# Recommender forward pass on one core: the next chunk's features loaded into X1's low half, a fourth weight slot, and three moves inside a step

## The reference

```python
target = item_id_feat + item_img_feat
x = concat([t, seq_emb, t - seq_emb, t * seq_emb], axis=-1)      # 50 history rows per item
weights = softmax(where(mask, -1e9, relu(x @ aw1 + ab1) @ aw2 + ab2), axis=1)
hist_feat = einsum('bs,bsd->bd', weights, seq_emb)
se = sparse * sigmoid(relu(z @ se_w1 + se_b1) @ se_w2 + se_b2)[:, :, None]   # 5 fields
vids = einsum('bfd,fde->bfe', se[:, :4], bil_W)
p = [vids[:, i] * se[:, j] for i in range(4) for j in range(i + 1, 5)]       # 10 pairs
dnn_in = concat([se, p])                                          # 15 features of 128
for i in range(2):                                                # cross_K is 2 x 1920 x 1920
    xc = dnn_in * (xc @ cross_K[i] + cross_bias[i]) + xc
h = gelu(ln(xc @ w1 + b1)); h = gelu(ln(h @ w2 + b2)); out = sigmoid(h @ w3 + b3)
```

## Time and profile before

| | |
|---|---|
| median of three runs | 2404.17 us |
| profiled execution, its span | 2398.13 us, 2396.1 us |
| TensorE busy | 2011.4 us, 84 % |
| VectorE, ScalarE, GpSimd busy | 1332.8, 902.6, 882.1 us |
| first product of chunk 0, 1, 2, 3 | at 403.2, 905.4, 1448.9, 1982.6 us |
| DMA | 220.33 MB, 92 GB/s over the span |

### The profile page before, as it was taken

How to read it: one execution, slowest core, us unless ns; L and a number is a source line. 1 busy time by engine, 2 the same in 40 slices (tenths; PEclk the granted TensorE clock), 3 DMA queues, 4 the chain that set the end, 5 groups by cost and what they waited for, 6 DMA issues and landing times. The chain is left out here.

```text
span 2396.1 us, 33252 instructions
## 1 busy us (share of the span) xinstructions
PE 2011.4 (84%) x9609; PEld 1554.4 (65%) x9609; DVE 1332.8 (56%) x2211; ACT 902.6 (38%) x1954; POOL 882.1 (37%) x854
## 2 busy tenths in 40 slices
PE   2654645999999988989989987989999988999995
PEld 1433433777766766767767766767767766888884
DVE  3434444576676644565676644566677644445542
ACT  1333322444444323554444323554444333322222
POOL 5666666565555500545565500445650000000000
PEclk6656565999999998999999998999999999999997
DMA  4111111334343442233343443233342343233330
GB/s 135 43 39 42 40 41 52 108 107 114 108 118 105 123 124 81 83 84 114 95 119 104 118 128 91 79 86 111 105 115 83 89 124 96 87 95 95 99 90 10
DMA packets 124354, 220.33 MB, mean 92 GB/s; under 512 B 22272, under 2 KB 50704, under 8 KB 124048
## 3 DMA queue, kind: packets, MB, share of 16 engines
q1 hardware_dynamic: 69440, 148.69, 20.9%
q0 software_dynamic: 27136, 55.63, 9.0%
q10 hardware_dynamic: 27600, 13.90, 2.1%
HBM read 205.27 MB, written 12.85 MB: 91 GB/s over the span
## 5 line engine op out<-in xcount | busy, mean ns | idle before, releaser
L386 POOL DMA_INDIRECT e<-in_item_table,idx_all x800 | 828.2, 1035 | 868.8 <-POOLq L404 386.3
L1011 DVE TENSOR_TENSOR Wl<-raw,Wh 128x640 fp32r<-128x640 f32 (+1 forms) x420 | 338.1, 805 | 315.4 <-DVEq L1010 287.4
L734 ACT ACTIVATE Wh<-raw 128x640 fp32r<-128x640 f32 (+1 forms) x420 | 300.5, 721 | 488.4 <-ACTq L733 427.2
L498 PE MATMUL xps<-X0h,Wh 128*128 128x512 f32 x900 | 375.2, 417 | 36.1 <-PEq L496 25.0
L498 PE MATMUL xps<-X1h,Wh 128*128 128x512 f32 x900 | 364.4, 405 | 11.6 <-PEq L492 6.3
L500 PE MATMUL xps<-X0h,Wl 128*128 128x512 f32 x900 | 360.8, 401 | 0.0
L499 PE MATMUL xps<-X0l,Wh 128*128 128x512 f32 x900 | 360.5, 401 | 0.0
L499 PE MATMUL xps<-X1l,Wh 128*128 128x512 f32 x900 | 354.5, 394 | 0.0
L500 PE MATMUL xps<-X1h,Wl 128*128 128x512 f32 x900 | 354.3, 394 | 0.0
L428 PE MATMUL aps<-ident,e 128*128 128x128 f32 x800 | 142.0, 318 | 173.7 <-issue 89.7
L702 ACT ACTIVATE e<-e,pw 128x128 f32<-128x128 f32 x800 | 242.7, 388 | 14.9 <-ACTq L128 11.7
(11 more groups left out here) (134 smaller groups left out, 2185.6 us busy)
## 6 DMA issues: line engine op xcount, KB each, us to landing
raw<-in_cross_K SPq DMA_DIRECT2D x360, 320.0 KB
raw<-in_w SPq DMA_DIRECT2D x60, 256.0 KB
e<-in_item_table,idx_all POOLq DMA_INDIRECT x800
dnn_scratch<-dn ACTq DMA_DIRECT2D x12, 960.0 KB
raw<-dnn_scratch SPq DMA_DIRECT2D x45, 256.0 KB
dn<-in_embT SPq DMA_DIRECT2D x1, 1024.0 KB
img_scratch<-dn ACTq DMA_DIRECT2D x1, 1024.0 KB, 5.2
S<-img_scratch ACTq DMA_DIRECT2D x16, 64.0 KB
```

The lines of the kernel that those rows point to most:

```text
L386: nc.gpsimd.indirect_dma_start(out=dst, out_offset=None, in_=table, in_offset=bass.IndirectOffsetOnAxis(ap=idx_all[:, t, s:s + 1], axis=0) ...
L498: m0 = mm(out, wh, Xh[:, k, 0:nb], start=(k == 0), stop=False)
L734: af(Wh[:, split_slot(w), 0:n], raw[:, rs, 0:n], ACT.Copy).then_inc(hi_done, 1)
L1011: v.tensor_tensor(Wl[:, rs, 0:n], raw[:, rs, 0:n], Wh[:, slot, 0:n].bitcast(F32), ALU.subtract).then_inc(lo_done, 1)
```

## The change

Six things change.

1. **Features.** `X1l` now lies on a float32 buffer `x1f`, and `X0l` on `x0f`, each with the layout [partition, tile, feature, item] where it was [partition, feature, 512 items]. A layer's new features are formed in place in `x1f` or `x0f`; `xnew` is gone. When the last feature of layer 1 is formed, X1 isn't needed any more, and ScalarE issues two loads (`rows_load`) that bring all 15 features of the next chunk to `x1f`: features 0 to 7 (2 MB) and 8 to 14. They are split from there by a table, two of them in w1 step 4, two in step 5, and so on. The SyncE queue carries weights alone.
2. **Layout.** The moving operand of every cross matmul is now four runs of 128 columns, and VectorE's and ScalarE's operations on a chunk are 128x4x128. A tile's store to DRAM and its high and low split in the opening are contiguous.
3. **Rings.** `RING` 3 to 4, `WRING` 5 to 6, and weights are split three blocks ahead, not two. The descriptor scratch of GpSimd goes from 8192 to 4096 bytes.
4. **Plan.** For tiles that are not in the opening: `fetch` at s-6, `aim` at s-4, `swing` at s-1 (the step without a group).
5. **TensorE's step.** `tail_turn` stands at the end of its step, `tail_bilinear` in the next step behind the first part. `fc_turn2` and `fc_w3` stand behind the second part.
6. **ScalarE's step.** `tail_copy` is first in the step after the turn, `tail_store` is last but for `fc_sd`, the head's second gelu stands behind the second copy of the group. On VectorE `fc_logits` stands one part later, and the low halves signal TensorE without a wait of VectorE on itself.

```diff
-RING = 3
-WRING = 5
+RING = 4
+WRING = 6
+LOOK = RING - 1
@@ make_plan
-        plan[s - 3].aim = plan[s - 2].swing = plan[s - 1].share = plan[s].neg = t
-        plan[max(s - 5, 0)].fetch = t
+        if t < TILES[0]:
+            fetch, aim, swing = max(s - 5, 0), s - 3, s - 2
+        else:
+
+            fetch, aim, swing = s - 6, s - 4, s - 1
+        plan[fetch].fetch = plan[aim].aim = plan[swing].swing = plan[s - 1].share = plan[s].neg = t
...
+LOADS = ((0, 8), (8, FEATS))
+SPLITS = {4: (0, 1), 5: (2, 3), 6: (4,), 7: (5,), 8: (6,), 9: (7,), 10: (8, 9), 11: (10,), 12: (11,), 13: (12,), 14: (13,)}
@@ build
-        dnn_d = nc.dram_tensor("dnn_scratch", (FEATS, P, ntiles, P), F32, kind="Internal").ap()
+        dnn_d = nc.dram_tensor("dnn_scratch", (ntiles, P, FEATS, P), F32, kind="Internal").ap()
-        X0l = sb("X0l", [P, FEATS, NB], F32R)
-        X1l = sb("X1l", [P, FEATS, NB], F32R)
+        x1f = sb("x1f", [P, TPC, FEATS, P])
+        x0f = sb("x0f", [P, TPC, FEATS, P])
+        X1l = nc.alloc_sbuf_tensor_at("X1l", [P, TPC, FEATS, P], F32R, offset=x_at)
+        X0l = nc.alloc_sbuf_tensor_at("X0l", [P, TPC, FEATS, P], F32R, offset=x_at + 4 * TPC * FEATS * P)
@@ TensorE, products
-                    m0 = mm(out, wh, Xh[:, k, 0:nb], start=(k == 0), stop=False)
+                    m0 = mm(out, wh, Xh[:, 0:T, k, :], start=(k == 0), stop=False)
@@ TensorE, step
                 products(p.chunk, p.layer, p.n, 0)
                 if T and 2 <= k < T + 2:
                     fc_turn1(k - 2)
-                if T and k == T + 3:
-                    fc_turn2(pairs(T)[0])
...
                 if p.open:
                     hidden()
-                if p.lift is not None:
-                    tail_turn(p.lift)
+                if p.pair is not None:
+                    tail_bilinear()
                 if p.grp:
                     transposes(*p.grp, 0)
 
                 products(p.chunk, p.layer, p.n, 1)
                 if p.grp:
-                    transposes(*p.grp, 1, p.swing is not None)
+                    transposes(*p.grp, 1)
                 elif p.swing is not None:
                     head_turn()
+                if T and k == T + 3:
+                    fc_turn2(pairs(T)[0])
...
                 products(p.chunk, p.layer, p.n, 2)
...
-                if p.lift is not None:
-                    tail_bilinear()
                 if p.open:
                     score()
+                if p.lift is not None:
+                    tail_turn(p.lift)
@@ ScalarE
+            def rows_load(c):
+                act.wait_ge(x1_free, 1).then_inc(x1_free, -1)
+                act.wait_ge(dnn_stored, DMA * (BASE[c] + TILES[c] - TILES[0]))
+                for i, (a, b) in enumerate(LOADS):
+                    act.dma_start(x1f[:, 0:TILES[c], a:b, :],
+                                  dnn_d[BASE[c]:BASE[c] + TILES[c], :, a:b, :].rearrange("t p f b -> p t f b")).then_inc(rows_landed[i], DMA)
@@ ScalarE, w1_stage
-                    if c + 1 < CHUNKS and k:
-                        r_hi(c + 1, k - 1)
+                    if c + 1 < CHUNKS:
+                        if k == 0:
+                            rows_load(c + 1)
+                        for r in SPLITS.get(k, ()):
+                            r_hi(c + 1, r)
@@ kernel
-    nc = bacc.Bacc("TRN2", target_bir_lowering=False, num_devices=1, dynamic_dma_scratch_size=8192)
+    nc = bacc.Bacc("TRN2", target_bir_lowering=False, num_devices=1, dynamic_dma_scratch_size=4096)
```

More of the change, by code:

```diff
@@ L269, in build @@
         w_free = sem("w_free")
-        r_free = sem("r_free")
+        x1_free = sem("x1_free")
+        rows_landed = [sem(f"rows_landed{i}") for i in range(2)]
         split_free = sem("split_free")
@@ L325, in build @@
         opening, chunks = make_plan()
-        order = load_order()
-        raw_slot = {item: i % WRING for i, item in enumerate(order)}
         TOTAL = CHUNKS * STREAM
@@ L337, in span, with by_tile, fresh @@
             return TILES[c] * P
+        def by_tile(x, c):
+            return x.rearrange("p (t b) -> p t b", b=P)[:, 0:TILES[c], :]
+        def fresh(c, layer, n):
+            return (x1f, x0f)[layer][:, 0:TILES[c], n, :]
         def e_sub(g, u, s):
@@ L355, in _ @@
             sp.dma_start(w2[:], w2_d.rearrange("(k p) n -> p k n", p=P)).then_inc(late_in, DMA)
[L356 to L358 removed]
+            for w in range(TOTAL):
+                if w >= WRING:
                     sp.wait_ge(w_free, 1).then_inc(w_free, -1)
[L360 to L371 removed]
+                b = w % STREAM
+                src = kx_d[b] if b < BLOCKS else w1_d[(b - BLOCKS) * P:(b - BLOCKS + 1) * P, :]
+                sp.dma_start(raw[:, raw_slot(w), 0:width(w)], src).then_inc(raw_landed[raw_slot(w)], DMA)
             sp.wait_ge(res_ready, 1).then_inc(res_ready, -1)
@@ L598, in step @@
                     fc_turn1(k - 2)
+                if p.open:
+                    hidden()
+                if p.pair is not None:
+                    tail_bilinear()
+                if p.grp:
+                    transposes(*p.grp, 0)
+                products(p.chunk, p.layer, p.n, 1)
+                if p.grp:
+                    transposes(*p.grp, 1)
+                elif p.swing is not None:
+                    head_turn()
                 if T and k == T + 3:
@@ L604, in step @@
                     fc_w3(T)
-                if p.open:
-                    hidden()
-                if p.lift is not None:
-                    tail_turn(p.lift)
-                if p.grp:
-                    transposes(*p.grp, 0)
-                products(p.chunk, p.layer, p.n, 1)
-                if p.grp:
-                    transposes(*p.grp, 1, p.swing is not None)
-                elif p.swing is not None:
-                    head_turn()
                 products(p.chunk, p.layer, p.n, 2)
@@ L799, in step @@
                     r_hi(c, FEATS - 1)
+                if p.pair is not None:
+                    tail_copy(p.pair)
                 unit(c, 3 * k)
@@ L817, in step @@
                     fc_gelu1(k - 2)
+                if p.grp:
+                    copy_eT(1)
+                elif p.swing is not None:
+                    copy_tT(p.swing)
                 if T and k == T + 3:
@@ L848, in _ @@
                 if p.k == 6:
-                    w_hi(0)
-                    w_hi(1)
+                    for w in range(LOOK):
+                        w_hi(w)
             for c in range(CHUNKS):
@@ L1136, in step @@
                 if prev:
-                    x_sum(c, prev[2])
+                    x_sum(*prev)
                 if p.summed:
@@ L1172, in step @@
                 unit_out(c, 3 * k + 2)
+                if T and k == T + 5:
+                    fc_logits(c - 1)
                 if p.gate is not None:
@@ L1202, in w1_stage @@
                         x_lo(c, 1, FEATS - 1)
-                    if c + 1 < CHUNKS and k:
-                        r_lo(c + 1, k - 1)
+                    if c + 1 < CHUNKS:
+                        for r in SPLITS.get(k, ()):
+                            r_lo(c + 1, r)
             dve.sem_inc(bank_free, BANKS)
@@ L1227, in _ @@
                 if p.k == 6:
-                    for w in range(2):
+                    for w in range(LOOK):
                         w_lo(w)
```

138 lines of the change are left out of this document (54 added, 84 removed).

## The result

| | before | after |
|---|---|---|
| median | 2405.28 us (2397.41 to 2407.41, 4 runs) | **2236.61 us** (2234.53 to 2242.17, 4 runs) |
| profiled execution, its span | 2398.13 us, 2396.1 us | 2237.56 us, 2235.5 us |
| first product of chunks 0, 1, 2, 3 | 403.24, 905.37, 1448.94, 1982.61 us | 408.72, 870.02, 1353.07, 1832.03 us |
| cross layers of chunks 0 to 3 | 443.2, 484.6, 474.6, 327.0 us | 420.5, 441.7, 438.2, 318.0 us |
| w1 stage to the next chunk's first product | 58.9, 59.0, 59.1 us | 40.8, 41.4, 40.8 us |

The ratio is 0.931 with the interval [0.928, 0.934]: 168.7 us faster, where 141 were forecast. The time lies just under the low end of the range, so what follows has to find some 28 us (168.7 less 141.1) that the sum had in no term.

What follows compares the result with a forecast made beforehand. GpSimd's gathers pace the opening; from 403 us TensorE decides, with 149 us of gaps. Terms summed to 141.1 us off the profiled 2398.1, giving 2257.0; with 6.0 for the median, 2263 us, range 2238 to 2320.

Steps and rivals of the forecast that it cites:

- w1 stages and chunk starts: TensorE's weight waits in w1 stages, 23.8 us gained; waits and slow matmuls at a chunk's first products, 37.6 us.
- turn: Steps 9, 15 and 21: nine TensorE waits for ScalarE's copy of the fields, with 49 slow matmuls, go; 37.7 us.
- store and target: Store last and `aim` a step earlier take 18 TensorE waits summing to 19.7 us; 16 us gained.
- one more weight: Splitting weights one block further ahead (the lookahead) removes weight waits inside steps; 20 of 21.8 us gained.
- head: `fc_turn2` behind the second part takes two waits and 6 slow matmuls, 7.7 us; 6 us gained.
- opening: Paced by GpSimd's gathers, unchanged; smaller scratch costs nothing, first product of chunk 0 still near 403 us.
- layout: 5400 cross matmuls reading their moving operand in four runs cost nothing; bounds zero to 2,600 us.
- rival A: Waits are moved, not removed: half of turn, store, one more weight and head comes back, 40 us; 2303 us, chance 0.16.
- The landing: First feature load on chip 20.2 us into the w1 stage, leaving TensorE about 0.5 us late for weight 8.
- Rival B: In w1 stages the feature loads starve the weights, 25 us a chunk, 75 in place of 4.5; 2333 us, chance 0.11.
- Rival C: Slower than before: TensorE pays for each jump in its moving operand; 2425 us at 10 ns a jump, chance 0.04.
- Rival D: No gain: TensorE's gaps are there for another reason than read; chance 0.02.

Runs made afterwards that it cites:

- features alone: Kernel before with the features' two large loads, layout, scratch 4096 and the low halves' new signal; rings, plan and step order as before: 2257.91 us, ratio 0.950.
- signal alone: Kernel before with one edit, the low half of a new feature (`x_lo`) signals TensorE itself: 2335.79 us, ratio 0.983.
- turn back: Kernel after with the fields transposed ahead of the group's transposes, their copy later, and the bilinear product at the step's end again: 2244.37 us, ratio 0.944.
- store back: Kernel after with the tile's store ahead of the second copy to `eT` again: 2217.37 us, ratio 0.933.
- plan back: Kernel after with `aim` at s-3, `swing` at s-2 and `fetch` at s-5 again: 2210.56 us, ratio 0.930.
- rings back: Kernel after with `RING` 3 and `WRING` 5, weights split two blocks ahead again: 2222.08 us, ratio 0.936.
- features and rings: Kernel after without the moves (also "no moves"): plan, turn, store and head order as before, features and rings as after: 2258.42 us, ratio 0.950.
- scratch 4096: Kernel before with GpSimd's descriptor scratch at 4096 bytes in place of 8192, nothing else: 2380.12 us, ratio 1.001.

## Why the prediction was right, and where its sum was off

Its picture of what bounds the kernel held: TensorE's gaps decided, the w1 stages lost theirs, the 5 us at a chunk's start and the waits at the turn in steps 9, 15 and 21 went, and no rival decided. Chunks 0 to 2 with their w1 stages are 156 us shorter, where under 100 would have been the sign of being wrong. The sizes are off in both directions, and one source of gain was missed.

| term | forecast, us | measured, us | from |
|---|---|---|---|
| w1 stages and chunk starts | 23.8 + 37.6 = 61.4 | 81 to 86 | features alone: 52.6 + 3 x 9.4, with or without 5 for the first groups |
| VectorE's own wait and signal behind `x_lo` | not priced | 38 | signal alone |
| turn | 37.7 | 33 | turn back |
| store and target | 16 | 4 one by one, 10 with the head | store back, plan back; turn back against no moves |
| one more weight | 20 | 9.5, or 0 without the moves | rings back, features and rings |
| head | 6 | its waits were moved, see rival A | |
| opening | 0 | some -5 | first products |
| layout | 0 | 0 | matmuls below |

The terms overlap and don't add up to the 162 us exactly: each "back" run measures a part with all others in. That the time came within 27 us of the forecast is in part luck: the first two rows were some 60 us too small together, and the turn, store, target, head, weight and opening some 30 us too large.

**The step that failed** is the list of parts: the signal of the low halves, in the change's sixth item, got no number at all, not even under Neutral. 30 steps a chunk x 3 chunks x 0.64 us are 58 us of VectorE's time, and 38 us of it lay on the path. The prediction charged VectorE's lateness at the softmax of the earlier trace rows to the store and to `aim` alone; the signal by itself takes eight of the 15 waits in steps 11, 17 and 23, and 6.6 of their 15.2 us. The lookahead's 20 shrank in part for the same reason: the wait for a weight in step 26 of chunk 0 is 2.16 us with scratch 4096 and 0.63 with the signal alone.

The Trainium skill, "VectorE: DVE Perf Modes", section "The DRAIN you can't avoid", would have supported the omission: it measures a chain of copies with a semaphore after each and only after the last at the same time, and says that "the semaphore costs nothing extra here". No row contradicts that for the increment: with it on the operation the next one starts 0.60 us later. What costs here is the wait of VectorE for its own operation and the signal given behind it, 0.64 us each time, and the measurement decides.

**The size of the first term.** A gap costs more than its idle time. This is one in the w1 stage of the kernel before:

```profile
860.42 0.39 PE L527 MATMUL xps<-Wh,X0l 128*128 128x512 f32 x1
861.01 0.47 PE L525 MATMUL xps<-Wh,X0h 128*128 128x512 f32 x1 [0.20 <-PEq L516]
861.31 0.39 PE L526 MATMUL xps<-Wl,X0h 128*128 128x512 f32 x1
```

A matmul's record is 0.39 us long at a pace of 0.23, so it overlaps its successor by 0.16, and that is lost at an idle time too; the matmul after it then comes 0.31 us later, the mean of 31 such places, and not 0.23. That makes 0.24 us a gap between products. (Behind a group of transposes the second product comes 0.31 us later with or without a wait, so there only the overlap counts.) The w1 stage with its 12 or 13 gaps of idle time had 9.4 us for weights, 1.2 for banks and 5.2 for the start, 15.8 in all, and 13 x 0.24 = 3.1 on top gives 18.9: it had lost 18.1 us (58.9 to 40.8). Over the chunks there were some 64 gaps fewer, an estimate of 10 to 15 us (at 0.16 to 0.24) that the forecast's list of gaps left out. With 118 us of idle time and 118 slow matmuls at 0.2 us (24 us) that accounts for 152 to 157 of the 165 us saved from the first product to the end of chunk 3's cross layers on the first chip.

**The landing.** The forecast had it 20.2 us into the stage and TensorE 0.5 us late; it was 13.7 us into it, and TensorE was never late. VectorE formed the last feature earlier, so the loads went out at 3.5 us in place of 6.3, and they took 10.2 us in place of 13.9, since the DMA engines moved 372 to 403 GB/s and not 284. That row was the fastest stretch of before, and nothing showed it to be a ceiling. The bank waits, expected to stay, went as well.

**Rival B** (starved weights) did not happen, but its mechanism is in the rows: ScalarE waited 4.43 and 2.50 us for weights. From 836 to 843 us weights got 0.59 MB, or 84 GB/s, against the 96 that they need. An estimate from the rule that the prediction takes from the Trainium skill ("DMA: Bandwidth & Descriptors", "Queues, rings and completion order") gives them a third of what is moved, here 134 of 403 GB/s. They got 21 %, while ScalarE stood waiting for them. So the estimate points the right way and gives too much; the total of 403 saved the stage. At 284 GB/s the same share would be some 60 GB/s, an estimate by which the weights would have run dry.

**Rival C** is out. TensorE with its moving operand in four runs (line 497, 2000 to 2150 us; busy us, mean ns, idle before):

```profile
L497 PE MATMUL xps<-X1l,Wh 128*128 128x512 f32 x221 | 86.0, 389 | 0.0
```

389 ns, and 0.23 us from start to start, as in one run before. **Rival D** is out. **Rival A** (half of turn, store, lookahead and head, 79.7 us, comes back): about a third did, by the 33, 10 and 9.5 us of the table. In the head its mechanism is in the rows. Before, `fc_turn2` waited in step 7 of chunk 1, and for 2.48 us in step 7 of chunk 2:

```profile
1036.46 0.63 PE L565 MATMUL xps<-ident,dn 128*128 128x128 f32 x4 [3.99 <-PEq L561]
```

After, the group's transposes wait in the same step for a copy of ScalarE, 3.46 us in chunk 1 and 3.06 in chunk 2; the longest wait left inside the steps is this one:

```profile
992.36 0.74 PE L426 MATMUL aps<-ident,e 128*128 128x128 f32 x5 [3.46 <-PEq L424]
```

That is 6.5 us in both kernels, and behind both stands VectorE, which reaches the group's softmax only after four normalisations of the head (at 1032.81 us before, 984.47 after). So these waits were moved and not removed.

**The opening** was forecast at 403, and was at 408.7, because the scratch was costed at nothing, on the argument that few gathers are open at a time. The scratch is the only edit of the kernel with 4096, and its first product is at 406.4. In the kernel after:

```profile
408.72 0.76 PE L496 MATMUL xps<-X0h,Wh 128*128 128x512 f32 x1 [6.69 <-PEq L494]
```

## What to carry to other kernels

Price every edit of an engine that hands work to and fro within a step, also the one that only changes how a signal is given: count the hand-overs, read the cost of one where nothing else is waited for, and take the product as the most that it can be worth. Take two edits back together as well as one by one when either could cover for the other. When a gap is read, look at the whole chain that was late and not at the last instruction in front of it, or one cause is paid out under several names. Count a gap as its idle time plus the restart, and look for a wait that is gone at the next instruction of the same step. Take the fastest DMA stretch of a profile as a floor of what is possible when little was asked for.

## What the runs showed of the hardware

- From one 128x512 operation of VectorE to the next it is 0.60 us when the first gives its signal itself, 0.84 with a wait for it in between, and 1.24 with the wait and a signal given apart.
- An idle time of TensorE between two products costs some 0.24 us beyond what the record shows, at the full clock.
- TensorE reads a moving operand in four runs of 128 columns at the pace of one: 389 ns, 0.23 us apart.
- The DMA engines moved 403 GB/s for 7 us, with two large loads beside the weights'; the weights got 21 % of it.
- GpSimd's gathers wait 35 times with a descriptor scratch of 4096 bytes, 25 or 26 times with 8192 or 2048.
